# Cross attention in one pipeline of five engines: another order of the steps on TensorE and on VectorE

## The reference, cut to what matters

```python
q = split_heads(layernorm(x) @ Wq.T + bq)        # 16 heads of 16
k = split_heads(ctx @ Wk.T + bk)
v = split_heads(ctx @ Wv.T + bv)
scores = einsum('bhqd,bhkd->bhqk', q, k) / 4
scores = where(mask == 0, -1e9, scores)
att = einsum('bhqk,bhkd->bhqd', softmax(scores), v)
x1 = x + layernorm(att + ctx) * gamma + beta
# layer 0's FFN: 8 experts, the best 2 for each row of layernorm(x1)
scores_BSN = layernorm(x1) @ Wr.T + br
```

## Time and profile before

| what | us |
|---|---|
| median of 3 runs (lowest, highest) | 966.21 (964.13, 966.92) |
| the profiled execution: its time | 958.49 |
| its span, first to last instruction | 956.6 |
| busy in the span: TensorE matmuls, weight loads | 864.7, 731.3 |
| busy: VectorE, ScalarE, GpSimd | 595.3, 467.7, 381.6 |
| mean granted TensorE clock | 0.973 of full speed |

### The profile page before, as it was taken

One profiled execution on the slowest core, in us unless ns is written; L12 is line 12 of the kernel. 1 busy time (PEld: TensorE's weight loads), 2 busy tenths in 40 slices (PEclk: granted clock), 3 DMA queues, 4 the chain that ended last, 5 costly groups with the idle time before them and its releaser, 6 DMA issues. The chain is left out here.

```text
span 956.6 us, 26657 instructions
## 1 busy us (share of the span) xinstructions
PE 864.7 (90%) x9044; PEld 731.3 (76%) x9045; DVE 595.3 (62%) x1484; ACT 467.7 (49%) x1194; POOL 381.6 (40%) x610
## 2 busy tenths in 40 slices
PE   5888888779999999997999899999999999689995
PEld 4676776549999999986566688888888887568784
DVE  3587887555545555542027476878678778459995
ACT  3788787422222222222343455445545454359894
POOL 4478887620000000007101346445555453436652
PEclk9999999789999999999999999999999999889997
DMA  6445656352333333316864597677687866212211
GB/s 167 131 153 164 188 164 213 130 209 70 119 96 108 95 99 95 96 39 204 291 204 149 140 186 170 144 158 177 138 170 138 176 134 124 62 35 64 66 52 46
DMA packets 190188, 128.27 MB, mean 134 GB/s; under 512 B 128545, under 2 KB 175649, under 8 KB 189985
## 3 DMA queue, kind: packets, MB, share of 16 engines
q1 hardware_dynamic: 155728, 93.72, 38.3%
q10 hardware_dynamic: 31312, 25.17, 9.3%
q0 software_dynamic: 3072, 8.39, 2.7%
HBM read 78.25 MB, written 48.99 MB: 133 GB/s over the span
## 5 line engine op out<-in xcount | busy, mean ns | idle before, releaser
L1763 ACT ACTIVATE c_pT<-c_T 128x512 f32<-128x512 f32 (+2 forms) x90 | 50.2, 595 | 101.9 <-PE c_T L1925 71.5
L1706 POOL TENSOR_TENSOR c_soft<-c_soft,c_share 128x616 f32<-128x616 f32 (+2 forms) x96 | 70.4, 762 | 60.6 <-DVE c_share L2181 59.0
L1094 ACT ACTIVATE b_rowsT<-b_RT 128x256 f32<-128x256 f32 x39 | 15.0, 385 | 152.8 <-PE b_RT L1136 152.8
L1716 POOL MEMSET d_round<- 128x1 f32 x1 | 0.1, 98 | 222.1 <-POOLq L981 222.1
L1145 PE MATMUL b_U<-b_rowsT,b_w 128*128 128x128 f32 x624 | 76.7, 277 | 0.0
L1222 DVE SCALAR_TENSOR_TENSOR b_hidT<-b_U,b_bias,b_gate 128x128 f32<-128x128 f32 x156 | 43.9, 344 | 52.5 <-PE b_U L1145 52.5
L1172 PE MATMUL b_Y<-moe_w,b_hidT 128*128 x312 | 73.9, 380 | 0.9 <-DVE b_out L1255 0.9
L1145 PEld LDWEIGHTS b_U<-b_rowsT,b_w 128*128 128x128 f32 x624 | 73.5, 194 | 0.0
L516 ACT ACTIVATE early<-a_S,early 128x128 f32<-128x128 f32 x256 | 70.7, 433 | 3.7 <-DVE early L796 3.7
L2039 PE MATMUL c_O<-early,c_attT 128*128 128x256 f32 x256 | 61.7, 396 | 5.0 <-ACT c_attT L1837 4.4
L1975 PE MATMUL c_T<-c_xT,early 128*128 128x128 f32 x512 | 61.0, 277 | 3.4 <-ACT c_kT L1763 2.4
(11 more groups left out here) (245 smaller groups left out, 2143.1 us busy)
## 6 DMA issues: line engine op xcount, KB each, us to landing
moe_w<-in_L_Wl SPq DMA_DIRECT2D x16, 512.0 KB
rel_windows<-c_relw ACTq DMA_DIRECT2D x28, 276.0 KB, 5.6
c_bias<-rel_windows SPq DMA_DIRECT2D x16, 462.0 KB, 5.0
prob_rows<-c_soft SPq DMA_DIRECT2D x16, 462.0 KB, 5.5
early<-in_L_early SPq DMA_DIRECT2D x16, 384.0 KB, 3.2
values<-c_pT ACTq DMA_DIRECT2D x22, 256.0 KB, 2.7
first_rows<-expert_lists SPq DMA_DIRECT2D x39, 128.0 KB, 2.6
expert_out<-b_out SPq DMA_DIRECT2D x39, 128.0 KB, 1.7
```

The costliest lines, as they stand in the source:

```text
L1706: ins = nc.gpsimd.tensor_tensor(soft[p][:, hs, a:z], soft[p][:, hs, a:z], share[:, s, hs].unsqueeze(2).to_broadcast([P, HS, z - a]), ALU.mult)
L1763: nc.scalar.activation(dst, view(T[k]), ACT.Copy, **kw).then_inc(g["emptied"], 1)
```

## The change

Two `steps` functions of `layer0` are reordered; no instruction is added, removed or altered, and the waits inside each step stay as they are. On TensorE `attention(b-2)` moves from the head of an iteration to behind `scores(b)` and the first two `probabilities(b-1)`, and `scores(b)` goes ahead of `probabilities(b-1, 0)`. On VectorE the two maxima stand in a row, right behind `norm_stats`; `denominators` and `attention_out` follow them; `out_rows` and `out_stats` go behind `choose_score`; `choose_index` goes ahead of `keys`, and `norm_rows(b+3)` is the last step.

```diff
--- before.py
+++ after.py
@@ -718,16 +718,15 @@
             transposes(1, 1)
 
             def steps(b, i, p):
-                if there(b - 2):
-                    attention(b - 2)
                 if there(b - 4):
                     places(b - 4, p)
-                if there(b - 1):
-                    probabilities(b - 1, 1 - p, 0)
                 if there(b):
                     scores(b, p)
                 if there(b - 1):
+                    probabilities(b - 1, 1 - p, 0)
                     probabilities(b - 1, 1 - p, 1)
+                if there(b - 2):
+                    attention(b - 2)
                 if there(b - 3):
                     next_rows(b - 3, 1 - p)
                 if there(b - 1):
@@ -891,8 +890,6 @@
 
             def steps(b, i, p):
                 front, ahead, behind, rows_ready, lists = there(b + 3), there(b + 1), there(b - 2), there(b - 3), there(b - 4)
-                if behind:
-                    den = denominators(b - 2)
                 if lists:
                     list_rows(b - 4, p)
                 if rows_ready:
@@ -901,30 +898,27 @@
                     list_slots(b - 4, i - 2, p)
                 if front:
                     stats = norm_stats(b + 3, i + 1 + p, 1 - p)
-                if behind:
-                    attention_out(den)
                 if there(b):
                     maxima(b, 0)
+                    maxima(b, 1)
+                if behind:
+                    den = denominators(b - 2)
+                    attention_out(den)
                 if front:
                     norm_var(stats)
-                if behind:
-                    rows = out_rows(b - 2, p)
-                if there(b):
-                    maxima(b, 1)
-                if behind:
-                    rows = out_stats(rows)
                 if rows_ready:
                     best = choose_score(b - 3)
                 if behind:
-                    out_var(rows)
-                if front:
-                    norm_rows(b + 3, 1 - p)
+                    rows = out_rows(b - 2, p)
+                    rows = out_stats(rows)
                 if rows_ready:
                     best = choose_best(best)
+                if behind:
+                    out_var(rows)
+                if rows_ready:
+                    best = choose_index(b - 3, 1 - p, best)
                 if ahead:
                     keys(b + 1, 1 - p)
-                if rows_ready:
-                    best = choose_index(b - 3, 1 - p, best)
                 if behind:
                     rows = rows_scaled(b - 2)
                 if rows_ready:
@@ -932,6 +926,8 @@
                 if behind:
                     rows_out(b - 2, i - 1, p, rows)
                     rows_stats(b - 2, p)
+                if front:
+                    norm_rows(b + 3, 1 - p)
 
             by_batch(steps)(dve)
             list_rows(NB - 1, 1)
```

## The result

The changed kernel takes **951.99 us** (median of four runs, 947.21 to 957.08); the kernel before, run beside it, 965.17 (959.15 to 966.92). The ratio is 0.9885, with a 95% interval of 0.9846 to 0.9924: 1.15% faster, some 11 us. Forecast were 953.8 us (12.4 us less) and a range of 948.5 to 962.5. The profiled execution takes 951.89.

What follows compares the result with a forecast made beforehand. Layer 0's attention was bound by a TensorE-ScalarE loop through oT. Gains of 0.6, 2.3, 5.0, 3.0 and 1.5 us, total 12.4, took 958.5 to 946.1; plus 7.7 to the median, 953.8 us, range 948.5 to 962.5.

Steps and rivals of the forecast that it cites:

- (a): TensorE: attention behind scores and two probabilities hides the 1.21 us oT wait, about 1.0 free; scores every 9.15 us.
- (b): VectorE: both maxima in a row, worth 0; the later reciprocal and attention_out stay hidden from TensorE by 1.8 us.
- (c): VectorE: rows_normal near the batch's start waits about 0.5 us for GpSimd's rstd2, then takes 0.81 beside the residual adds.
- V: The end of VectorE's var2 in a batch; rows_normal was to start 1.05 us after it.
- (d): VectorE: norm_rows last saves 0.33 us between out_var and rows_scaled; its later DMA and keys behind choose_index cost 0.
- Rival 3: VectorE's rows_normal loses the shared port to both GpSimd adds and takes 1.5 us: period 10.35, 961.8 us; chance 0.14.
- what is late next: Counted loop: GpSimd at 9.66 us and VectorE at about 9.4 mesh, giving 9.65 a batch where GpSimd has all its work.
- rival 5: VectorE's chain holds both GpSimd round trips in series: up to 11.0 us a batch, deciding from 10.6; 969.7 us; chance 0.08.
- Batches 13 to 15: Stage's last batches, without masks or new rows: TensorE and ScalarE's loop rules at 9.2 instead of 10.24, gaining 3.0 us.
- loop (a): TensorE and ScalarE's loop from scores through probabilities, copies and exponentials to the next scores, put at 9.15 us a batch.
- Drain: End of the attention stage: probabilities fill TensorE's 3.54 us wait for oT, gaining 1.5 us (bounds 0 and 2.5).

Runs made afterwards that it cites:

- e10: Kernel before plus one idle 128x512 ScalarE copy per batch, ahead of the first exponentials: 978.59 us, 1.0144 of the kernel before.
- e2: Changed kernel with VectorE's old order put back, TensorE's new order kept: 961.89 us, 0.9978 of the kernel before.
- e4: Changed kernel with norm_stats moved ahead of rows_normal, into VectorE's wait for rstd2: 0.9893 of the kernel before.
- e6: Changed kernel with norm_stats ahead of rows_normal and the add of beta moved from GpSimd to VectorE: 0.9908 of the kernel before.
- e7: Kernel before, unaltered, traced a second time: the first expert tile's transposes start at 216.2 us, in the first trace at 209.9.
- e8: Kernel before, unaltered, traced a third time: the first expert tile's transposes start at 215.2 us, in the first trace at 209.9.
- e11: Changed kernel plus one idle 128x512 ScalarE copy per batch: 957.53 us, 0.9918 of the kernel before.

## Why the prediction held, and where it did not

**The bound before: right, and stronger than told.** The loop oT, `attention`, `probabilities` 0, `scores`, copies, exponentials set the pace. Batches 2 to 4 of e10 show it from the other side.

**(a), TensorE's order: right.** The wait is 0.0 instead of 20.7, `attention` starts 2.19 after `scores` (forecast 2.2), and batches 2 and 3 take 9.17 and 9.29 (8.95). One hand-over is mis-sized, the end of the exponentials. ScalarE and then TensorE at the end of batch 3:

```profile
50.41 2.26 ACT L516 ACTIVATE early<-a_S,early 128x128 f32<-128x128 f32 x8
52.40 0.75 ACT L527 ACTIVATE a_oT<-a_T 128x512 f32<-128x512 f32 x1
```

```profile
52.81 0.40 PE L628 MATMUL a_S<-a_masked,a_ones 32*128 32x512 bf16 x4 [0.72 <-ACT early L516]
```

I had the exponentials end where oT starts, and `scores` 0.05 to 0.08 behind. They end at 52.67, 0.27 after oT starts, and `scores` follows 0.41 after that start; the earlier trace rows show the same, 122.29 + 2.26 = 124.55 for oT at 124.30. That 0.3 is the excess of batch 3: 4.39 to the first exponential, 4.49 to oT, 0.41. The prediction did not say that this part needs VectorE's; e2 shows it.

**(b), the maxima in a row: right in its covers.** TensorE waits for `att` 1.1 us in the whole stage. What had no price is how late the end of VectorE's batch has become for TensorE: `keys` was put at 0 by VectorE's wait for its input alone, and hot was not named. TensorE waits 0.30 and 0.28 a batch for them. The prediction named a wait of `scores` for keys as the sign that VectorE is later than I have it; the wait stands at the transposes (L590) two steps ahead of `scores`, and says the same.

**(c), `rows_normal` behind rstd2: right in kind, small in size.** It waits 0.63 to 0.86 in the counted loop (0.5), starts 1.28 after V, not 1.05, and lasts 0.71 (0.81). `norm_rows` at the end, (d), costs nothing and no longer waits. Rival 3, the port lost to both adds, is out: the first add ends at 114.88 and the operation at 115.03 already.
The Trainium skill ("SBUF — State Buffer", section "SBUF: two separate sides") has the loser blocked for the whole instruction. These rows don't bear that out to the letter: blocked until 114.88, it would need its 0.41 after that, and be over at 115.29, unless it can do a part of the 0.41 while it is blocked, which no run here separates. The row that the prediction called in agreement is the same: 185.53 + 0.81 is 0.16 after the add's end. At the end of the changed kernel's stage it is over 0.16 after the add as well, and takes 0.41 with no add beside it (188.22). GpSimd's spans are rough by the profile's own word, so the 0.3 between may be theirs.

**The step that failed is "what is late next": 9.65.** Measured are 10.03 to 10.05. I had two loops below it, GpSimd at 9.66 and VectorE at 9.4, and said that they mesh. VectorE's is mis-sized by 0.65. From out_var's start to var2's end I had 3.1; measured are 3.38 (119.71 to 123.09), because `rows_scaled` and the next operation take 0.61 and 0.63 (0.47 and 0.48 before the change). From V to out_var's start that leaves 6.3, measured 6.67: 0.23 in the wait for rstd2, and the rest where dependent instructions now stand next to each other (L803, L807; L815, L819, L823), each 0.10 after the end of the one before, where independent ones start 0.08 ahead of it. That is rival 5's chain with the round trip for rstd2 bare and that for rstd1 behind `keys`, at 10.05 rather than 10.7: below its point of decision. GpSimd's, by e4, is mis-sized by 0.37 to 0.42; 0.26 of that is L439 at 0.46, 0.05 the second add at 0.78. Longer operations beside another engine's were priced for one of them, not for the short ones. GpSimd is busy 8.66 of 10.01, 87%, where I wrote over 90%. Batches 4 to 12 thus gain 2.6 over the first trace, not 5.0. A third loop, e6's, was not seen at all. (By its own numbers, 9.6 against 10.18 and 9.2 against 10.24, the prediction's 5.0 and 3.0 should read 5.2 and 3.1.)

**Batches 13 to 15: half right.** 9.74 and 9.86, forecast 9.2. `scores` does end on loop (a), as forecast: it waits 0.41 and 0.54 for the exponentials, while var2 to var2 takes 9.25 and 9.59 (143.02, 152.27, 161.86). It is longer than I had it by the same 0.3 behind the exponentials, and by 0.3 to 0.4 ahead of them, where ScalarE waits 0.47 and 0.58 for the transposes of new rows.

**Drain: mis-sized.** It was to bring 1.5 and brought nothing (43.0 before, 43.2 after, means of three from scores(15)). With batches 13 to 15 it was to bring 4.5; b_RT is 1.1 nearer to scores(13) by the means, and not at all between the first traces (63.2, 63.3). TensorE's 3.54 is used, but VectorE meets both round trips, 0.92 to 0.94 and up to 1.65, each batch: what was hidden in a full queue is bare in an empty one.

**Why the total came within 1.8 us all the same.** (The second measurement of the changed kernel, 955.61, lies as far on the other side.) I took 12.4 off the profiled 958.5, then added the 7.7 that stand between it and the median, as a thing of the run that the change leaves alone. Part of it is not: e7 and e8 end the stage 6.3 and 5.3 later than the first trace did, and the changed kernel shows nothing of the kind (205.3, 203.3, 203.1). Between the first traces the stage gains 4.6 of the 12.4; between the means of three 9.9, which is 1.0% of 965, where the runs measure 1.08 to 1.15%. The 5.3 between these two is made of 2.6 in batches 4 to 12, where the late copies lie, 1.6 ahead of them, in part the clock from 20 to 28 us, and 1.2 behind them. So a good part of what pace and drain failed to bring was made up by things that I did not know of. The sign stood on the mechanism; how near the number came was luck.

## What to carry to other kernels

When a wait of one engine is removed, lay out every loop that closes over a batch, with each hand-over at its measured length, and expect the next ones to be near: here three seem to lie within 0.15 us of each other, and single edits, and even three at once, gave nothing. Take two or three traces of the kernel before: one execution that runs smoothly hides what the others lose, and the gain is against those. To show that an engine is in the loop, add idle work to it in both kernels, and read the answer batch by batch: the total may hold more than the work added, as in e10.

## What the runs showed of the hardware

- ScalarE's copies out of a_M start 0.5 to 1.3 late in some batches of some executions (in e7 at 102.07, 1.26 after the copy before, for transposes over at 101.25), with nothing in the trace that releases them late. Cause open; nothing was tried on it.
- A short GpSimd operation takes 0.40 or 0.24 (L415), 0.46 or 0.20 (L439), by what VectorE does beside it, it seems; nothing was tried on it. VectorE's `rows_normal` takes 0.41 alone, 0.71 to 0.81 beside the adds.
- Extra ScalarE work in e10 came with a granted clock of 0.93 in the batch at 105 us and 0.90 in the two ahead of it (79.6 to 92.1, 92.1 to 105), where e11 has 1.00 from 28 to 150 us, so a part of those 14 us may be TensorE's. It was not separated.
